# An attention kernel's order of work: the next batch's statistics, projections and stack loads in the first third of a batch

## The reference, cut to what matters

```
x: 8 x 512 x 128                      # 8 batches of 512 tokens
x = x + attn(layernorm(x))            # attention layer
x = x + ffn(layernorm(x))             # 8 experts, top 2 per token

attn(x): h = rmsnorm(x, norm_w); q, k, v = h@Wq, h@Wk, h@Wv      # 16 heads of 8
  lin = causal linear attention, second order feature map of q@Wqf, k@Wkf, over v
  win = softmax(q k^T / sqrt(8), window of the last 64 keys) v
  out = x + concat(lin, win) @ Wout
ffn(x): softmax of x@gate_W, top 2; experts 0-3 gelu MLPs, 4-7 KAN layers;
  weighted sum of the two chosen experts
```

## Time and profile before

| | us |
|---|---|
| three runs | 1186.19, 1187.79, 1195.24 |
| median | 1187.79 |
| span of the profiled execution | 1192.4 |
| TensorE matmuls busy in the span | 887.9 (74%) |
| ScalarE, VectorE, GpSimd busy | 552.5, 521.9, 509.1 |
| attention phase, first L1371 to its last steps | about 57 to 645 |

### The profile page before, as it was taken

One profiled execution on the slowest core, in us unless ns is written; L12 is line 12 of the kernel. 1 busy time (PEld: TensorE's weight loads), 2 busy tenths in 40 slices (PEclk: granted clock), 3 DMA queues, 4 the chain that ended last, 5 costly groups with the idle time before them and its releaser, 6 DMA issues.

```text
span 1192.4 us, 24590 instructions
## 1 busy us (share of the span) xinstructions
PE 887.9 (74%) x8106; PEld 675.3 (57%) x8107; DVE 521.9 (44%) x2114; ACT 552.5 (46%) x744; POOL 509.1 (43%) x647
## 2 busy tenths in 40 slices
PE   2087897968889698898950277777699988996871
PEld 1055675646656466665630145446487877886770
DVE  5161735527364262736322011112466666575440
ACT  1275563636556364665610142332566565474440
POOL 6050433425333252534133648774445554462222
PEclk9599898979989798998975588898798988998886
DMA  2504032130503204040101245556133241242113
GB/s 55 81 2 73 6 84 23 61 46 2 95 11 78 29 28 78 2 96 9 29 27 25 47 76 76 89 78 163 49 90 90 62 123 46 56 118 64 38 11 86
DMA packets 96202, 68.64 MB, mean 58 GB/s; under 512 B 42892, under 2 KB 87114, under 8 KB 94730
## 3 DMA queue, kind: packets, MB, share of 16 engines
q1 hardware_dynamic: 79210, 55.36, 20.7%
q0 software_dynamic: 16832, 11.09, 6.8%
HBM read 46.86 MB, written 21.37 MB: 57 GB/s over the span
## 4 chain that ended last, share of the span: by engine, by line
PE 32%; POOL 18%; issue 17%; DMA 13%; DVE 6%; ACT 6%; SPq 5%; POOLq 1%; another core or an unknown queue 1%; DVEq 0%; ACTq 0%
POOL acc_d L751 8%; DMA stack<-zeros 6%; PE pv L1449 5%; PE pv L1636 5%; DMA acc_d<-stack,srec 4%; PE ring L1609 4%; PE ring L1371 2%; PE ring L1391 2%; ACT Pb L851 2%; PE ring L1460 2%; PE ring L1412 2%; ACT stack L928 2%; DVE masked L1050 2%; PE ring L1416 2%; POOL stack L741 1%
## 5 line engine op out<-in xcount | busy, mean ns | idle before, releaser
L751 POOL DMA_INDIRECT acc_d<-stack,srec x84 | 136.3, 1623 | 136.8 <-DVE stack L1237 98.1
L1050 DVE CUSTOM_DVE_ANT_0 masked<-ring,mask_max 128x192 bf16<-128x192 f32 (+1 forms) x512 | 141.6, 337 | 114.4 <-PE ring L1371 102.4
L1248 DVE SCALAR_TENSOR_TENSOR stack<-stack 128x512 f32<-128x512 f32 x240 | 158.0, 690 | 43.8 <-ACT stack L928 29.1
L692 POOL TENSOR_SCALAR_AFFINE_SELECT Pb<-Pb 128x1024 f32<-128x1024 f32 x64 | 69.0, 1094 | 218.9 <-ACT Pb L851 160.0
L928 ACT ACTIVATE stack<-ring,kprm 128x512 f32<-128x512 f32 x160 | 111.2, 794 | 107.7 <-DVE stack L1248 105.5
L1449 PE MATMUL pv<-Pb,vaug 128*16 128x128 f32 (+3 forms) x2816 | 142.7, 329 | 22.8 <-issue 22.6
L1636 PE MATMUL pv<-stack 128*128 128x128 f32 x1120 | 136.0, 285 | 17.0 <-DVE stack L1248 9.7
L1636 PEld LDWEIGHTS pv<-stack 128*128 128x128 f32 x1120 | 132.9, 200 | 20.9 <-DVE stack L1248 10.6
L1609 PE MATMUL ring<-stack 128*128 128x256 f32 x560 | 136.9, 409 | 6.0 <-issue 3.8
L1609 PEld LDWEIGHTS ring<-stack 128*128 128x128 f32 x560 | 115.3, 208 | 30.2 <-issue 7.7
L857 ACT ACTIVATE Pb<-ring 128x768 f32<-128x768 f32 x128 | 101.2, 812 | 56.9 <-PE ring L1400 55.6
(11 more groups left out here) (204 smaller groups left out, 1279.7 us busy)
## 6 DMA issues: line engine op xcount, KB each, us to landing
stack<-L_ffn_kan_sl_W SPq DMA_DIRECT2D x20, 1024.0 KB
stack<-hl_d SPq DMA_DIRECT2D x72, 128.0 KB
Pb<-L_ffn_mlp_W SPq DMA_DIRECT2D x22, 256.0 KB
hl_d<-hi SPq DMA_DIRECT2D x7, 384.0 KB, 2.3
hl_d<-lo SPq DMA_DIRECT2D x7, 384.0 KB, 2.9
xb<-L_attn_x SPq DMA_DIRECT2D x9, 256.0 KB
acc_d<-res SPq DMA_DIRECT2D x8, 256.0 KB, 2.5
h_d<-h SPq DMA_DIRECT2D x8, 256.0 KB, 3.1
```

The costliest lines, as they stand in the source:

```text
L751: pool.indirect_dma_start(acc_d, bass.IndirectOffsetOnAxis(ap=srec[:, kind, u, q, 0:1], axis=0), src[:, u % 2, q, :], None, compute_op=ALU ...
L1050: red = dve.tensor_tensor_reduce(masked[:, (NT * n + c) % SLOTS, hh, k0:WQ], slot(job)[:, hh // 2, WQ * (hh % 2) + k0:WQ * (hh % 2 + 1)], ...
L1248: dve.scalar_tensor_tensor(basis[z][:, g % G, :], s_, -1.0, s_, ALU.add, ALU.mult).then_inc(k_bas[z], 1)
```

## The change

The words of `ORDER` for the front of the next batch move. Places are counted from 0 in the list of 93 words.

| word | place before | place after |
|---|---|---|
| stats, aggr, coef | 25, 27, 29 | 0, 3, 6 |
| hT, q, k | 43, 49, 51 | 19, 25, 30 |
| u, v, stacks | 63, 64, 69 | 34, 37, 40 |
| out, coef2 (tail) | 16, 21 | 20, 26 |
| h2norm, h2T, logit (tail) | 40, 44, 47 | 46, 49, 52 |
| mT, store, first W | 52, 56, 60 | 55, 59, 63 |
| residual, xload, scatter | 70, 81, 91 | 70, 81, 91 |

SyncE's share becomes stacks, mT, store, xload; GpSimd's becomes masks, coef, coef2, residual, scatter in that order of the words. GpSimd waits in "residual" for one more semaphore, since coef2 no longer stands ahead of coef on its queue.

```
 ORDER = """
-M L M L M -ytr L M L M L -ycT M L M M -out L L L M -coef2 L M L +stats M +aggr P +coef L L M L L M L
-M M L -h2norm P L +hT -h2T M L -logit L +q L +k mT Y L L -store P L -choose W W W +u +v -rank P
--total W +stacks +residual W -gapexp W W P W Y W W -weights +xload P W W W W Y W W P -scatter P
++stats M L +aggr M L +coef M -ytr L M L M L -ycT M L M M +hT -out L L L M +q -coef2 L M L +k M P L +u L M +v L L
++stacks M L M M L -h2norm P L -h2T M L -logit L L mT Y L L -store P L -choose W W W -rank P
+-total W +residual W -gapexp W W P W Y W W -weights +xload P W W W W Y W W P -scatter P
 """.split()
...
                     if s == "residual":
 
                         pool.wait_ge(x1_stored[1 - u % 2], i * 16 + ((u + 1) // 2 * 16 + LEAD_DMA))
+                        if u:
+                            pool.wait_ge(n2_ready, batch_no(i, u, 1, 0))
                         pool.sem_inc(pool_at, 1)
                         residual(1 - u % 2)
```

## The result

| | before | changed |
|---|---|---|
| median, us (4 runs each) | 1189.42 | 1273.78 |
| lowest to highest | 1186.19 to 1195.24 | 1269.61 to 1279.11 |
| ratio, 95% interval | | 1.072 [1.067, 1.077] |
| span of the profiled execution | 1192.4 | 1271.4 |
| from batch 0's start to batch 7's | 485.1 | 568.4 |

The change costs 84 us, 7%. The forecast was 1256, range 1222 to 1291, slower with a chance of 0.88: direction and cause held, the forecast was 18 us too low. All of the loss lies in the seven batches that have a next batch to prepare.

A forecast was written before the change was run, and what follows sets the result against it. TensorE's in-order queue was taken to set the pace. Wait for mT 68, clock 15, hn 7, gains -22 made +68: 1260 us against the span, 1256 against the median, range 1222 to 1291.

The forecast's parts named there:

- The wait before the first W step: TensorE's first W waits for mT, which lands when the stack load does: 9.8 us in batches 0 to 6, +68.
- The prediction's other reading: On SyncE's queue, half of a transfer issued behind the load moves at once, the busy engines' half after the load.
- The clock: After the wait before the first W step: 4 us of work at half speed, 2.1 us lost, seven times, +15.
- hn: TensorE's hT step, now straight ahead of out, waits 1 us for hn, seven times: +7.
- The stacks: At a batch's start the stacks are already there, so TensorE's named waits for them go: -13.8 us.
- The jumps: TensorE's 14.3 us of idle time at the loop's two jumps lie partly beside the load: -4 us.
- Starved of instructions under the load: The load running under L, M and P steps would not starve TensorE of instructions: costed at nothing.
- mT passing the load: Rival at the first W's wait: mT lands 17.4 us after u, ahead of TensorE; -15, 1173 us, chance 0.08.
- a TensorE too slow to notice: Rival: TensorE needs 25 us from u to the first W, so the wait is 3 us; 1194 us, chance 0.04.

The follow-up runs named there:

- the other chip: The changed kernel, unchanged, run on the last group's chip beside the kernel before: 1.067 [1.060, 1.074] of before.

## Why the prediction was right, and where its sum was off

- **The wait before the first W step** (68 us): right in place, in count and in what ended it, measured 54.0. TensorE's own time from u was 18.8 in batch 3, predicted 18.4. What was mis-sized is the landing: 26.7 us after u instead of 28.2 in batch 3. At its old place the load ran beside the scatter and the x load, at the new one beside the output stores; which of them makes the 1.5 us was not tested. Over the seven batches the wait was 5.2 to 10.1 us, 7.7 in the mean, against 9.8. That the load stands ahead on SyncE's queue was not needed: from another queue the row lands no sooner. The prediction's other reading, that half of a later transfer moves at once and the other half after the load, is what the packets of that run show.
- **The clock** (15 lost, 4 gained, 11 net): measured 20.7 us more busy time. No run shows the 4 us gained as a term of their own. The seven waits cost 13 to 14, by the run with stacks moved back, as estimated. By the trace's clock record the clock was low for 78.9 us of the stretch before and for 134.9 changed. Of these, 61.5 lie around the seven waits. What the runs showed in their place: the low stretch around the start of batch 1 (115.4 to 125.6, 10 us long) is gone, and the other low stretches are no shorter, 65 us before and 66 now.
- **hn** (7 us more): 8.4 against 3.3 before, 5.1 more. The sum fits better than its parts: the scatter did not land in 7.42 us, the select followed it by 8.6 to 9.7 us, and half of the total is one wait of 4.09. On the other chip it is 23.2.
- **The stacks** (-13.8): right, all gone. **The jumps** (-4): nothing; 10.7 before, 10.8 after.
- **The term that was missing.** The prediction held that ScalarE and VectorE only do the same work at another time, at no cost. In the first third VectorE is busy with the M steps; lo of k and of u comes late, the PSUM slot is held, and TensorE, at most three steps ahead, waits: 6.3 + 4.9 us (DVEq L991), and 3.9 us for ScalarE ahead of q. The same two rows, 6.3 and 4.9, stand in the run with stacks moved back. Neither stands in a kernel with the projections at their old places, the one with only stats early included, so they come with the early projections. That VectorE's busy first third makes them was argued from the rows, not tested by itself.
- **Starved of instructions under the load** (nothing): right; the total of such waits didn't grow (19.9 us of "issue" at the P steps before, 19.0 after).
- **The rivals**: mT passing the load did not happen, nor did a TensorE too slow to notice.

The sum with measured terms: 54.0 + 20.7 + 5.1 + 11.2 + 3.9 - 13.8 + 0 = 81.1, against 83.3 in the stretch; the smaller rows left out make up the rest. The remainder of the kernel took 4.2 less in this pair of profiles, which is within what the runs scatter. That the forecast came within 18 us is in part luck: the wait was put 14 us too high, while the clock, the missing term and the jumps together were put 29 us too low.

The prediction speaks of five rows with an idle time before a batch's first matmul and lists six; no number hangs on the count.

## What to carry to other kernels

A big load moved earlier also moves ahead of every small transfer that is issued while it runs, and here a small transfer landed only when the load ended (11.23 us after its issue in batch 3, against 2.3), and another queue did not help (12.5). So before moving a load, list the small transfers with a waiter in the window it will occupy, and start it right behind the last of them, only as early as its own length asks. And when the wait that a change removes is gone, look at what stood ready behind it: here the next batch ran into GpSimd's scatter, and the projections at their new places into the three PSUM slots.

## What the runs showed of the hardware

- The shift row of 16 KB took 12.5 us to land from ScalarE's queue beside SyncE's load, and 2.1 to 2.3 us with no load in flight. Beside the load 8 of its 16 packets moved some 1.3 us after the issue, the other 8 as the load ended.
- Six transfers of 8 or 16 partitions instead of nine of 8 doubled the DMA share (0.58 to 1.20, in the stretches compared) and the packets under way (9.0 to 18.4), with 255 ns a packet instead of 145, and raised the rate only from 65 to 74 GB/s; the load with its wait became 17.6 instead of 20.9 us long.
- The same kernel showed two pictures of a batch's end on two chips: the last P steps in dribbles (idle times of about 1 us put down to "issue", 19.9 us over the seven batches) or in one piece. Its medians were 1189 and 1160 us there, but most of that difference lies outside these batches.
